# Local attention in blocks of 32 queries by 64 keys, in a six-layer transformer kernel

## The chip, the cores and the metric

The kernel runs on one core of a Trainium2 chip. The metric is the device time of one execution in microseconds (us). TensorE (PE) does the matrix products, ScalarE (ACT) activations and copies out of PSUM, VectorE (DVE) elementwise work and reductions, GpSimd (POOL) elementwise work, and the queue of SyncE (SP) issues the DMAs. PSUM has eight banks of 128 partitions by 512 fp32.

## What is computed

Eight batches of 512 tokens of 128 features pass through a full causal attention block with a layer norm, then through six layers of local attention and a gated feed-forward block, then a last layer norm. The change touches only the local attention of the six layers, 16 heads of 64 features:

```python
w = 32
bk2, bv2 = look(bk), look(bv)          # each block of 32 queries sees its own 32 keys and the 32 before
mask = (it < jb) | (it > jb + w) | (jb == -1)
sim = einsum('bhwie,bhwje->bhwij', bq, bk2) * 8.0
attn = softmax(where(mask, -max, sim), -1)
out = einsum('bhwij,bhwje->bhwie', attn, bv2)
```

A query sees itself and the 32 tokens before it, no more than 33 keys.

## The kernel before

After a first stage of about 480 us the six layers run as one software pipeline. An iteration n is one batch of one layer (48 in all); it has eight steps p = 0 to 7. A step handles a "pair": one group of four heads (a quarter of the heads) and half of the tokens (256). So there are 384 pairs. Each engine runs its own hand-written order, `cycle(n, p)`, and semaphores tie them. In step p different pairs are at different stages: the projection works on the pair of this step, the transposes of queries and keys on the pair of two steps ago (LAG_T), logits and softmax on that of four steps ago (LAG_S), transposes of the probabilities six (LAG_PT), products with the values and the output projection seven (LAG_O, LAG_Y). The feed-forward block of an older iteration (n-2) is spread over the steps: a turn at p = 2, `up` products at p = 3, 4, 6 and 7, 24 `down` products at p = 5; DVE has its layer norm at p = 0 and 1.

PE in one step, in order, with the lines of its matmuls: projection of queries and keys of the first 128 tokens (L1019 to L1021), transposes of half of the probabilities (`transpose_probs`, hp = 1, L1082), products with the values (`outputs`, L1103), logits (mask products L1118, then L1125), transposes of queries and keys (L1057), projection of the second 128 tokens (L1019 to L1021), value projection (L1031 to L1033), transposes (L1057), output projection (L1143), transposes of the other half of the probabilities (hp = 0, L1082).

Logits are made in blocks of 64 queries by 96 keys (KW = 96, so that 64 queries with their 32 older keys fit). A pair has 16 such blocks (4 heads, 4 blocks of queries). They lie in two banks as 128 partitions x 2 x 384. An fp32 matmul is recorded as two matmuls with a weight load (PEld) each, so L1125 has 32 in a step. The 64 x 64 tiles of PE that the blocks use are the four quadrants of the array. DVE takes the maxima of 128x768 (`maxima`, L1714), ACT the exponentials in eight instructions of 128x96, each with a sum (`exps`, L1441), DVE the reciprocals (L1772), POOL the products of probabilities and reciprocals (`probs`, 128x384 twice, L1564). The result PN is padded to 128 columns for each 64 queries, so two heads' blocks give one transpose of 128x128, eight in a step, in two groups of four in banks `p_ta` and `p_tb`; ACT copies each group to PT (128x512, L1402). `outputs` multiplies blocks of 64 columns of PT with values: V_odd holds the values as they were projected (128 keys), V_even a copy moved by 64 partitions by DMA (96 keys), 16 fp32 matmuls of 64 columns into one bank, `p_vo`. ACT copies that to OT (L1409).

Two loops close over a step. The logits have one pair of banks, so the masks of a pair wait until ACT has taken all eight exponentials of the pair before (`exp1`). And ACT, in its order, does: copy of probabilities (hp = 1), outputs, squares (L1417), copy of queries and keys (L1424), squares, four exponentials, copy of queries and keys, values (L1432), copy of probabilities (hp = 0), four exponentials.

Of the kernel before, what the change touches and what calls it, by code (L numbers as in the profile page):

```python
# [14 lines left out]
F32 = mybir.dt.float32  # L15
# [7 lines left out]
T = 512  # L23
# [12 lines left out]
KW = 3 * WIN  # L36
# [71 lines left out]
def first_attention(nc, dram, X, ident, banks, w, A, S, X0, kept, late):  # L108
# [3 lines left out]
    with ExitStack() as ctx:  # L112
# [56 lines left out]
        with nc.Block() as block:  # L169
# [230 lines left out]
            def _(dve):  # L400
# [18 lines left out]
                def step(b, j, odd):  # L419
# [90 lines left out]
                    if b == 7 and j == F_X + 1:  # L510
                        dve.tensor_copy(A["masks"][:, :, :], masks_f[:, :, 0:2 * KW])
                        dve.tensor_copy(A["ident_b"][:, :], ident[:, :])
# [124 lines left out]
def layer_constants(nc, ctx):  # L637
# [10 lines left out]
    sb("masks", [P, 2, 2 * KW], BF16)  # L648
# [5 lines left out]
def late_buffers(nc, ctx, A):  # L654

    both = ctx.enter_context(nc.sbuf_tensor("late", [P, 2 * NF * T + 2 * T + 6 * CQ + 16 * P + 4 * CQ + 16 * KW], F32))
# [12 lines left out]
    A["PT"] = view("layers", 16 * P, "p (s n q) -> p s n q", s=2, n=8)  # L669
    A["OT"] = view("layers", 4 * CQ, "p (s e t) -> p s e t", s=2, e=2)  # L670
# [5 lines left out]
def layer_buffers(nc, ctx, made):  # L676
# [16 lines left out]
    for n in ("V_even", "V_odd"):  # L693
        sb(n, [P, G, MT, CQ])
    sb("PN", [P, 2, 4, 2 * P])
# [41 lines left out]
def all_layers(nc, X, X0, out, ident, psum, banks, A, w, dram, S, kept, late):  # L737
# [7 lines left out]
    QK, V_even, V_odd, E, PN, negmax, esum, erec, PT, OT = (  # L745
        A[n] for n in ("QK", "V_even", "V_odd", "E", "PN", "negmax", "esum", "erec", "PT", "OT"))
# [4 lines left out]
    p_qk, p_vo, p_ta, p_tb, p_y = banks[0:2], banks[2], banks[5], banks[6], banks[7]  # L751
    p_t = (p_ta, p_tb)
    p_s = psum[:, 3:5, 0:4 * KW]
# [3 lines left out]
    end_gates, end_values, end_out = (banks[2], banks[4], banks[7]), (banks[5], banks[6], banks[0]), (banks[3], banks[1])  # L757
# [26 lines left out]
    with nc.Block() as block:  # L784

        @block.sync
        def _(sp):
            moved = {}

            def move_values(a):  # L790
# [4 lines left out]
                sp.dma_start(V_even[WIN:KW, a.g, m:m + 2, :], V_odd[0:64, a.g, m:m + 2, :]).then_inc(S[name], 16)  # L795
                later = slice(m + 1, min(m + 3, MT))
                sp.dma_start(V_even[0:WIN, a.g, later, :], V_odd[KW:P, a.g, later.start - 1:later.stop - 1, :]).then_inc(S[name], 16)
# [101 lines left out]
        def _(pe):  # L899
            def transpose_x(n):  # L900
# [3 lines left out]
                ge(pe, S["pt_out1"], done(n - 1, P_X, LAG_PT))  # L904
# [52 lines left out]
            def up(n, p, c, part, bank):  # L957
                f = n - 2
                if 0 <= f < NI:
# [3 lines left out]
                    else:  # L963
                        pe.wait_ge(S["pt_out1"], done(n, p, LAG_PT))
# [32 lines left out]
            def shifts(n):  # L997
                l = prepared(n)
                if l is not None:
                    ge(pe, S["w1"], 32 * l)  # L1000
                    ge(pe, S["pt_out1"], done(n, P_BIAS, LAG_PT))
# [34 lines left out]
            def transpose_qk(n, p, mm):  # L1036
                t = pair_at(n, p, LAG_T)
                if t:
                    f = n - 2
                    pe.wait_ge(S[f"r{mm}"], t.k + 1)  # L1040
                    ge(pe, S[f"pt_out{mm}"], done(n, p - (mm == 0), LAG_PT))
# [18 lines left out]
            def transpose_probs(n, p, hp):  # L1060
                t = pair_at(n, p, LAG_PT)
                if t:
                    f = n - 2
                    pe.wait_ge(S[f"pn{hp}"], t.k + 1)
                    pe.wait_ge(S[f"qk_out{hp}"], done(n, p - hp, LAG_T))
                    if hp == 0:
# [1014 lines left out]
```

## Time and profile before

| | |
|---|---|
| time of three runs | 3645.51 us median (3644.78 to 3646.31) |
| span of the profiled execution | 3639.9 us |
| PE, ACT, DVE, POOL busy | 3554.4, 3359.9, 3128.2, 2732.9 us |
| granted clock of PE | 9 tenths or more in all 40 slices |
| the pipeline of layers | 48 iterations of 65.6 us, eight steps each |

The page gives busy time by engine, the chain that ended last, and groups of instructions by line. The matmul records overlap each other (a matmul of 0.24 us can be followed by another 2 ns later), so a busy share of 98% says little of the rate; the chain of waits gives each group the time that it added.

### The profile page before, as it was taken

The numbers are of one execution on the slowest core, as the hardware profiler recorded it, in microseconds if no ns is written. First come the engines' busy times: TensorE is split into PE (matmuls) and PEld (weight loads), VectorE is DVE, ScalarE is ACT, GpSimd is POOL, SyncE is SP. The second block draws the span as 40 slices with busy tenths as digits, with TensorE's granted clock in tenths as the row PEclk, the third lists the DMA queues.
The fourth block names the chain that finished last, engine by engine and source line by source line (L and its number), as shares of the span: only waits on it lengthen the run. The fifth ranks groups of instructions, "written<-read, shape, count | busy, mean of one in ns | idle before, by whom it ended". The sixth has DMA issues, their size and how long they took to land.

```text
span 3639.9 us, 133048 instructions
## 1 busy us (share of the span) xinstructions
PE 3554.4 (98%) x47348; PEld 3028.6 (83%) x47348; DVE 3128.2 (86%) x7021; ACT 3359.9 (92%) x10928; POOL 2732.9 (75%) x2058
## 2 busy tenths in 40 slices
PE   8999999999999999999999999999999999999998
PEld 5666678888888888888888888888888888888887
DVE  8999988888888788887888888889888888888887
ACT  8999889999999999999999999999999999999996
POOL 0111288888888788788888888888888888888884
PEclk9999999999999999999999999999999999999999
DMA  2000011111111111111111111111111111111111
GB/s 102 7 14 10 14 38 43 35 32 34 44 43 41 28 36 36 39 46 36 33 33 40 40 45 35 33 30 43 47 35 37 30 33 45 34 35 36 42 36 39
DMA packets 165015, 132.71 MB, mean 36 GB/s; under 512 B 113933, under 2 KB 124813, under 8 KB 164109
## 3 DMA queue, kind: packets, MB, share of 16 engines
q1 hardware_dynamic: 164365, 124.19, 13.9%
q8 instruction: 390, 6.39, 0.8%
q14 instruction: 260, 2.13, 0.2%
HBM read 25.84 MB, written 4.19 MB: 8 GB/s over the span
## 4 chain that ended last, share of the span: by engine, by line
PE 75%; ACT 5%; DVE 4%; issue 3%; POOL 1%; ACTq 0%; POOLq 0%; DVEq 0%
PE bank L1103 10%; PE bank L1057 10%; PE bank L1082 8%; PE bank L1143 8%; PE bank L1125 6%; PE bank L1019 4%; PE bank L1020 4%; PE bank L1021 4%; PE bank L980 4%; PE bank L1118 3%; PE bank L953 2%; ACT late L1441 2%; PE bank L955 2%; PE bank L954 2%; PE bank L1033 2%
## 5 line engine op out<-in xcount | busy, mean ns | idle before, releaser
L1554 POOL TENSOR_TENSOR a_rn<-a_ssqc,a_minus_half 128x16 f32<-128x16 f32 x384 | 1113.2, 2899 | 490.3 <-DVE a_ssqc L1765 480.6
L1441 ACT ACTIVATE late<-bank,a_negmax 128x96 f32<-128x96 f32 x3072 | 1013.5, 363 | 11.8 <-DVE a_negmax L1714 10.7
L1577 POOL TENSOR_TENSOR a_r<-a_u,a_rn 128x512 f32<-128x512 f32 x768 | 788.3, 1046 | 0.6
L1564 POOL TENSOR_TENSOR a_PN<-late,a_erec 128x384 f32<-128x384 f32 x768 | 730.6, 971 | 9.1 <-PE bank L1082 8.2
L1441 ACT ACTIVATION_READ_ACCUMULATOR late<-bank,a_negmax 128x1 f32 x3072 | 708.7, 231 | 0.0
L1424 ACT ACTIVATE a_QK<-bank 128x512 f32<-128x512 f32 x768 | 467.8, 609 | 122.5 <-PE bank L1057 122.5
L1737 DVE TENSOR_TENSOR a_v<-bank,a_rot_s 128x512 f32<-128x512 f32 x768 | 523.1, 681 | 0.0
L1727 DVE TENSOR_TENSOR a_u<-bank,a_rot_c 128x512 f32<-128x512 f32 x768 | 521.4, 679 | 1.2 <-ACT a_sq L1417 1.1
L1417 ACT ACTIVATE a_sq<-bank 128x512 f32<-128x512 f32 x768 | 482.7, 628 | 42.2 <-PE bank L1021 12.9
L1402 ACT ACTIVATE late<-bank 128x512 f32<-128x512 f32 x758 | 479.6, 633 | 15.3 <-PE bank L1082 11.4
L1745 DVE TENSOR_TENSOR a_u<-a_u,a_v 128x1024 f32<-128x1024 f32 x384 | 489.5, 1275 | 0.7 <-issue 0.3
L1057 PE MATMUL bank<-ident,a_r 128*128 128x128 f32 x3072 | 482.4, 280 | 3.5 <-DVE a_xl L1646 2.3
L1757 DVE TENSOR_REDUCE a_ssq<-a_sq 128x16 f32<-128x1024 f32 x384 | 463.9, 1208 | 17.4 <-issue 16.7
L1082 PE MATMUL bank<-ident,a_PN 128*128 128x128 f32 x3072 | 461.2, 273 | 9.1 <-DVE X L1672 7.5
L1082 PEld LDWEIGHTS bank<-ident,a_PN 128*128 128x128 f32 x3072 | 367.2, 141 | 75.3 <-issue 30.0
L1714 DVE TENSOR_REDUCE a_negmax<-bank 128x8 f32<-128x768 f32 x384 | 365.1, 951 | 64.7 <-PE bank L1125 64.7
L1143 PE MATMUL bank<-w_out,late 128*128 128x128 f32 x3072 | 406.0, 275 | 0.0
L1103 PE MATMUL bank<-late,a_V_even 96*64 96x64 f32 x6144 | 397.6, 227 | 4.9 <-DVE late L1871 2.8
L1057 PEld LDWEIGHTS bank<-ident,a_r 128*128 128x128 f32 x3072 | 341.2, 141 | 64.8 <-issue 3.9
L1103 PE MATMUL bank<-late,a_V_odd 128*64 128x64 f32 x6144 | 379.1, 221 | 0.0
L1143 PEld LDWEIGHTS bank<-w_out,late 128*128 128x128 f32 x3072 | 373.4, 192 | 0.7 <-ACT late L1409 0.4
L1103 PEld LDWEIGHTS bank<-late,a_V_even 96*64 96x64 f32 x6144 | 310.3, 137 | 70.1 <-ACT late L1402 34.3
(191 smaller groups left out, 8129.7 us busy)
## 6 DMA issues: line engine op xcount, KB each, us to landing
a_V_even<-a_V_odd SPq DMA_DIRECT2D x384, 128.0 KB, 2.3
a_V_even<-a_V_odd SPq DMA_DIRECT2D x192, 64.0 KB, 2.2
late<-in_qkv SPq DMA_DIRECT2D x20, 384.0 KB, 3.8
a_x_sh<-X SPq DMA_DIRECT2D x48, 128.0 KB
a_V_even<-a_V_odd SPq DMA_DIRECT2D x192, 32.0 KB, 1.9
a_x_sh<-X SPq DMA_DIRECT2D x48, 127.0 KB
late<-X SPq DMA_DIRECT2D x47, 128.0 KB
late<-X SPq DMA_DIRECT2D x47, 127.0 KB
```

Source lines behind the costliest of these rows:

```text
L1057: ins = pe.transpose(p_t[mm][:, c * P:(c + 1) * P], r[:, t.par, mm * 512 + c * P:mm * 512 + (c + 1) * P], ident[:, :])
L1082: ins = pe.transpose(p_t[hp][:, i * P:(i + 1) * P], PN[:, t.par, 2 * hp + i // 2, first:first + P], ident[:, :])
L1103: ins = pe.matmul(p_vo[q, hp * CQ + i * 64:hp * CQ + (i + 1) * 64], V[:, c:c + DH], PT[keys, o.par, 4 * hp + i, side:side + 64], start=Tru ...
L1143: ins = pe.matmul(p_y[:, i * P:(i + 1) * P], OT[:, y.par, hp, mm * P:(mm + 1) * P], w.out[:, 2 * y.g + hp, :], start=(y.pos + hp == 0 and ...
L1417: act.activation(sq[:, mm * 512:(mm + 1) * 512], p_qk[mm][:, :], ACT.Square).then_inc(S[f"sq{mm}"], 1)
L1441: ins = act.activation(E[:, s.par, k, :], scores[:, i % 2, col:col + KW], ACT.Exp, bias=negmax[:, s.par, k:k + 1], accum_out=esum[:, s.par ...
L1554: pool.tensor_tensor(rn[:, a.par, :], ssqc[:, a.par, :], minus_half[:, :], ALU.pow).then_inc(S["rn"], 1)
L1564: pool.tensor_tensor(PN[:, s.par, 2 * hp:2 * hp + 2, :].rearrange("p i (b k) -> p i b k", b=2)[:, :, :, 0:KW], spread(E[:, s.par, half, :] ...
L1577: pool.tensor_tensor(heads(r[:, a.par, half]), heads(u[:, a.par, half]), rn[:, a.par, mm * 2 * HG:(mm + 1) * 2 * HG].unsqueeze(2).to_broad ...
L1727: dve.tensor_tensor(view(u[:, a.par, mm * 512:(mm + 1) * 512]), view(p_qk[mm][:, :]), tab, ALU.mult).then_inc(S["u_rot"], 1)
L1737: dve.tensor_tensor(halves(v[:, mm * 512:(mm + 1) * 512]), halves(p_qk[mm][:, :])[:, :, :, ::-1, :], tab, ALU.mult).then_inc(S[f"v_rot{mm} ...
L1745: dve.tensor_tensor(u[:, a.par, :], u[:, a.par, :], v[:, :], ALU.add).then_inc(S["u"], 1)
```

## The change

KW becomes 64: logits are blocks of 32 queries by 64 keys, 32 blocks in a pair, each in a tile of 64 rows by 32 columns of the array. They take 128 partitions x 2 x 256 of PSUM, even heads in one bank and odd heads in the other. Masks are eight bf16 products of 32 rows by 256 columns. Maxima, exponentials and probabilities get two thirds of the elements, with the same number of instructions. PN is [128, 4, 128] without padding: each 128x128 block, four in a step, is transposed once, into `p_ta` alone; one copy by ACT gives PT. `outputs` has 32 fp32 matmuls of 64 keys by 64 features by 32 queries, in the four quadrants of the array; the results of keys in the lower 64 partitions go to `p_vo`, the others to `p_tb`, and ACT copies both banks in one instruction. `p_vo` and `p_ta` exchange banks. The values lie in V_nat (as projected) and V_sh (moved down by 32 partitions by DMA): the first of two DMAs for a pair moves 96 partitions instead of 64.

```diff
-KW = 3 * WIN
+KW = 2 * WIN
...
-                sp.dma_start(V_even[WIN:KW, a.g, m:m + 2, :], V_odd[0:64, a.g, m:m + 2, :]).then_inc(S[name], 16)
+                sp.dma_start(V_sh[WIN:P, a.g, m:m + 2, :], V_nat[0:P - WIN, a.g, m:m + 2, :]).then_inc(S[name], 16)
...
+            def prob_transposes(t):
+                for k in range(4):
+                    ins = pe.transpose(p_ta[:, k * P:(k + 1) * P], PN[:, t.par, k, :], ident[:, :])
+                ins.then_inc(S["pt"], 1)
...
+                    pe.wait_ge(S["qk_out1"], keys_out)
                     ge(pe, S["o_out"], o.k)
...
                     for hp in range(2):
-                        for i in range(4):
-                            keys = slice(0, P if i % 2 else KW)
-                            V = (V_odd if i % 2 else V_even)[keys, o.g, 2 * o.half + i // 2, :]
-                            for e in range(2):
-                                q, c, side = slice(64 * e, 64 * e + 64), hp * P + 64 * e, 64 * ((e + i) % 2)
-                                ins = pe.matmul(p_vo[q, hp * CQ + i * 64:hp * CQ + (i + 1) * 64], V[:, c:c + DH],
-                                                PT[keys, o.par, 4 * hp + i, side:side + 64], start=True, stop=True)
+                        for c in range(4):
+                            m, own = divmod(c, 2)
+                            V, col = V_nat if own else V_sh, hp * P + c * WIN
+                            for half in range(2):
+                                keys = slice(KW * half, KW * half + KW)
+                                for e in range(2):
+                                    q, v = slice(64 * e, 64 * e + 64), hp * P + 64 * e
+                                    ins = pe.matmul(p_o[half][q, col:col + WIN], V[keys, o.g, 2 * o.half + m, v:v + DH],
+                                                    PT[keys, o.par, 2 * e + hp, c * WIN:(c + 1) * WIN], start=True, stop=True,
+                                                    skip_group_check=True)
...
+                    for c in range(4):
+                        for e in range(2):
+                            rows = slice(WIN * c, WIN * c + WIN)
+                            pe.matmul(scores[rows, e, :], ident_b[sides[e], 64 * e:64 * e + WIN],
+                                      masks[sides[e], int(s.half > 0 or c > 0), :], start=True, stop=True, skip_group_check=True)
                     for hp in range(2):
...
+                        for half in range(2):
+                            col = (2 * hp + half) * KW
+                            for c in range(4):
+                                first = (2 * s.half + c // 2) * P + half * KW + c % 2 * WIN
+                                for e in range(2):
+                                    ins = pe.matmul(scores[WIN * c:WIN * c + WIN, e, col:col + KW],
+                                                    QK[sides[e], s.gpar, hp, WIN + first:WIN + first + WIN],
+                                                    QK[sides[e], s.gpar, 2 + hp, first:first + KW], start=False, stop=True,
+                                                    skip_group_check=True)
...
                 project(n, p, 0)
-                transpose_probs(n, p, 1)
-                outputs(pair_at(n, p, LAG_O), n * NP + p)
+                if p == P_GELU + 1:
+                    ge(pe, S["f_out"], n - 2)
+                outputs(pair_at(n, p, LAG_O), n * NP + p, done(n, p - 1, LAG_T))
...
                 transpose_qk(n, p, 1)
+                transpose_probs(n, p)
                 output_projection(pair_at(n, p, LAG_Y))
-                transpose_probs(n, p, 0)
...
-                probs(t, 1)
+                squares(n, p, 0)
                 outputs(o)
-                squares(n, p, 0)
...
-                probs(t, 0)
+                probs(t)
```

Where PE waited for `pt_out1` before writing `p_tb` (transposes of keys, `up`, x), it now waits for `o_out`. The last steps, written out one by one in `end()`, follow the same rules.

## Rows read from the trace of the kernel before

**Rows 1.** The page: span, busy time, and the granted clock in 40 slices.

```profile
span 3639.9 us, 133048 instructions
PE 3554.4 (98%) x47348; PEld 3028.6 (83%) x47348; DVE 3128.2 (86%) x7021; ACT 3359.9 (92%) x10928; POOL 2732.9 (75%) x2058
...
PEclk9999999999999999999999999999999999999999
```

**Rows 2.** The page: the chain that ended last, share by engine.

```profile
PE 75%; ACT 5%; DVE 4%; issue 3%; POOL 1%; ACTq 0%; POOLq 0%; DVEq 0%
```

**Rows 3.** The chain of waits over one step (start, time added, what), step p = 0.

```profile
2069.33 0.44 PE bank L1082 x4
2069.76 1.08 PE bank L1103 x32
2070.85 0.29 PE bank L1118 x8
2071.14 0.66 PE bank L1125 x32
```

**Rows 4.** Timeline of PE (start, us, what): step p = 0 and the next masks.

```profile
2068.38 0.48 PE L1019 MATMUL bank<-a_wh,a_xh 128*128 128x512 f32 x1
...
2069.69 0.34 PE L1103 MATMUL bank<-late,a_V_even 96*64 96x64 f32 x4
...
2070.78 0.36 PE L1118 MATMUL bank<-a_masks,a_ident_b 64*64 64x192 bf16 x8
...
2071.73 0.66 PE L1057 MATMUL bank<-ident,a_r 128*128 128x128 f32 x4
...
2075.31 0.48 PE L1019 MATMUL bank<-a_wh,a_xh 128*128 128x512 f32 x1
...
2076.62 0.34 PE L1103 MATMUL bank<-late,a_V_even 96*64 96x64 f32 x4
...
2077.81 0.36 PE L1118 MATMUL bank<-a_masks,a_ident_b 64*64 64x192 bf16 x8
```

**Rows 5.** Windows of 5 ns on L1125's matmuls: stretch, length, busy, running (x).

```profile
2004.94:2004.95 0.01, 0.01 (x4) 1.00 0.23 51
2004.96:2004.96 0.01, 0.01 (x8) 1.00 0.00 0
2005.02:2005.03 0.01, 0.01 (x8) 1.00 0.23 51
2005.04:2005.05 0.01, 0.01 (x12) 1.00 0.23 51
```

**Rows 6.** Timeline of PE: matmuls of one column, then the projection.

```profile
507.51 1.25 PE L1006 MATMUL bank<-w_cols,w_w 128*128 128x1 f32 x12
508.62 0.48 PE L1019 MATMUL bank<-a_wh,a_xh 128*128 128x512 f32 x1
```

**Rows 7.** Timeline of ACT over the same step as rows 4.

```profile
2072.42 0.60 ACT L1424 ACTIVATE a_QK<-bank 128x512 f32<-128x512 f32 x1 [0.41 <-PE bank L1057]
2073.12 0.60 ACT L1417 ACTIVATE a_sq<-bank 128x512 f32<-128x512 f32 x1
2073.61 0.33 ACT L1441 ACTIVATE late<-bank,a_negmax 128x96 f32<-128x96 f32 x1
...
2074.87 0.62 ACT L1424 ACTIVATE a_QK<-bank 128x512 f32<-128x512 f32 x1
...
2076.30 0.39 ACT L1441 ACTIVATE late<-bank,a_negmax 128x96 f32<-128x96 f32 x1
```

**Rows 8.** Busy time by engine: steps p = 7, 0, 1, then p = 5, 6.

```profile
2060.40:2082.50 22.10, 22.07 (x334) 19.76 (x333) 21.84 (x44) 20.50 (x74) 18.95 (x15) 1.00 0.19 46
2041.30:2060.40 19.10, 18.66 (x250) 16.37 (x248) 12.54 (x20) 17.86 (x52) 13.85 (x10) 1.00 0.12 28
```

**Rows 9.** Groups by line from 600 to 3500 us: busy, mean ns, idle before.

```profile
L1714 DVE TENSOR_REDUCE a_negmax<-bank 128x8 f32<-128x768 f32 x353 | 335.7, 951 | 58.1 <-PE bank L1125 58.1
L1757 DVE TENSOR_REDUCE a_ssq<-a_sq 128x16 f32<-128x1024 f32 x353 | 426.5, 1208 | 16.8 <-issue 16.1
```

More of the change, by code:

```diff
@@ L647, in layer_constants @@
         sb(n, [P, MT, 2, DH])
-    sb("masks", [P, 2, 2 * KW], BF16)
+    sb("masks", [P, 2, 4 * KW], BF16)
     sb("ident_b", [P, P], BF16)
@@ L692, in layer_buffers @@
     sb("QK", [P, 2, 4, XC])
-    for n in ("V_even", "V_odd"):
+    for n in ("V_sh", "V_nat"):
         sb(n, [P, G, MT, CQ])
-    sb("PN", [P, 2, 4, 2 * P])
+    sb("PN", [P, 2, 4, P])
     for n in ("negmax", "esum", "erec"):
@@ L903, in transpose_x @@
                 ge(pe, S["h"], NF * (n - 3) + 1)
-                ge(pe, S["pt_out1"], done(n - 1, P_X, LAG_PT))
+                ge(pe, S["o_out"], done(n - 1, P_X, LAG_O))
                 for i in range(MT):
@@ L963, in up @@
                     else:
-                        pe.wait_ge(S["pt_out1"], done(n, p, LAG_PT))
+                        pe.wait_ge(S["o_out"], done(n, p, LAG_O))
                     if part == 0:
@@ L1000, in shifts @@
                     ge(pe, S["w1"], 32 * l)
-                    ge(pe, S["pt_out1"], done(n, P_BIAS, LAG_PT))
+                    ge(pe, S["o_out"], done(n, P_BIAS, LAG_O))
                     pe.wait_ge(S["xl"], n + 1)
@@ L1040, in transpose_qk @@
                     pe.wait_ge(S[f"r{mm}"], t.k + 1)
-                    ge(pe, S[f"pt_out{mm}"], done(n, p - (mm == 0), LAG_PT))
+                    if mm == 0:
+                        ge(pe, S["pt_out"], done(n, p - 1, LAG_PT))
+                    else:
+                        ge(pe, S["o_out"], done(n, p, LAG_O))
                     if n == 0:
@@ L1286, in end_outputs @@
             def end_outputs(j):
-                outputs(end_pair(j), NI * NP)
+                outputs(end_pair(j), NI * NP, NI * NP + min(0, j + 5))
             def end_projection(j):
@@ L1329, in end @@
                 end_up(0, 1)
+                end_probs(-1)
                 end_projection(-2)
-                end_probs(-1, 0)
                 end_up(1, 1)
@@ L1984, in _ @@
             end()
-LAYER_SEMS = ("xt xh xl x_loaded f_loaded qk_out0 qk_out1 pt0 pt1 pt_out0 pt_out1 v_out o_out o y pn0 pn1 exp0 exp1 logits r0 r1 "
+LAYER_SEMS = ("xt xh xl x_loaded f_loaded qk_out0 qk_out1 pt pt_out v_out o_out o y pn0 pn1 exp0 exp1 logits r0 r1 "
               "qkt0 qkt1 sq0 sq1 qk v max red u u_rot rec0 rec1 rn v_rot0 v_rot1 summed x_out weights w_hi w_lo raw0 raw1 scales "
```

171 lines of the change are left out of this document (64 added, 107 removed).

## The prediction

> **What bounds the kernel now.** I read the page first, then the chain of waits, then one step on each engine. The page [rows 1] shows PE busy 98% of the span at an undiminished clock and ACT at 92%: two engines without reserve. The chain [rows 2] is PE for 75%. But matmul records overlap, so the price of a PE group has to come from the time that it adds to the chain [rows 3]: transposes of probabilities 0.44 us for each group of four (two groups a step), products with the values 1.08, masks and logits 0.29 + 0.66. Together 2.91 us of a plain step (p = 0) of 6.93 us, which is the distance of the two first L1019 [rows 4].
>
> A second bound lies close behind. From one pair's masks to the next are 7.03 us [rows 4], and this can be walked through ACT [rows 4, 7]: masks to transposes of keys 0.95 (2070.78 to 2071.73), to their copy on ACT 0.69, to the squares 0.70 (they wait for the projection), to the first exponential 0.49, four exponentials 1.26, copies of keys, values and probabilities 1.43, and from the second four to the next masks 1.51. The sum is 7.03: the masks wait for `exp1` and nothing else is slack. The masks start 1.19 us after the first product with the values at p = 1 (2076.62 to 2077.81) and 1.09 at p = 0 [rows 4]: only the former waits 0.1 us for the exponentials. The other steps repeat one of these, p = 2 to 4 the former and p = 5 to 7 the latter, so I count four turns as bound by the loop and four by PE.
>
> A third is DVE. Over steps p = 7, 0 and 1, where it also has the norm's statistics and the last residual sums, it is busy 21.84 of 22.10 us; over p = 5 and 6 only 12.54 of 19.10 [rows 8].
>
> **The change, part by part, per step.**
>
> Transposes of probabilities. One group of four of two goes: 0.44 us of PE [rows 3]. The tile change before the outputs is still there, it only follows the projection. The group that stays is moved ahead of the output projection, which costs nothing by itself; what queues behind it (projection, in step 5 the `down` products) needs it done either way. One ACT copy of 128x512 goes too; it stood between `exp1` and the squares, where ACT then waits 0.41 us for keys anyway [rows 7], so I cost it at nothing. If that wait closed, it would be worth up to 0.48.
>
> Logits. The 32 recorded matmuls of 96 columns become 64 of 64 columns. The price depends on how many the array runs at once. Windows of 5 ns [rows 5] show the matmuls start in groups of four: 4 records are open at 2004.94 and 8 some 0.01 us later, still 8 at 2005.02 and 12 at 2005.04. So four start within about 0.01 us and then none until the next four; 8 such rounds are the 0.66 of [rows 3], 0.082 us each, with one matmul in each quadrant. Four starts close together after a pause mean that the array, not the issue of instructions, sets the pace. 0.082 us for 96 columns; by proportion 0.055 for 64. With tiles of 64 rows by 32 columns there is room for eight at once, and the written order takes all eight tiles in turn: 64 / 8 = 8 rounds of 0.056 = 0.45, a saving of 0.21. If only four run at once it is 16 rounds, 0.90, a loss of 0.24. No row shows eight tiles. I take eight, because the rounds of [rows 5] are already full, one matmul in every tile that exists there, and keep both ends.
>
> Masks. Eight matmuls of 192 columns take two rounds (0.19 us between the L1118 and L1125 starts, about 0.11 and 0.08). Eight of 256 columns in eight tiles take one, about 0.13: 0.05 saved; two rounds of four would take 0.24: 0.05 lost.
>
> Products with the values. 32 recorded matmuls of 64 columns become 64 of 32 columns, two tiles at once become four. Each still loads 64 columns of weights, and a load has its price where matmuls have one column [rows 6]: 12 of them, eight with 128 and four with 85 columns of weights (the chunks of 341), take 1.11 us, 0.81 ns a column, so 64 columns 0.052 and about 0.058 with what is between two. Now 16 rounds of 0.058 make 0.93 of the 1.08; afterwards 64 / 4 = 16 rounds, bound by the load instead of the matmul, 0.93 again: no change. That loads of four tiles overlap follows from [rows 5]: 4 x 0.052 would not fit in 0.082. The upper end is a round of 0.082, the slowest that four tiles show: 16 x 0.024 = 0.38 more. Below zero it can't go far, as the loads bound it.
>
> PE in sum: -0.44 - 0.21 - 0.05 = -0.70, with ends -0.80 (a cheaper tile change) and +0.23.
>
> A rule of the Trainium skill speaks against this. The page "TensorEngine Tiling (Array Packing)", section "Instruction Overhead", says that each matmul carries about 60 cycles, that one of a single column takes as long as one of 60, and that a tiling factor shouldn't be taken from a dimension that is small already. An estimate from that page's figure is 64 x 25 ns = 1.6 us for the outputs and as much for the logits, against 0.93 and 0.66 now. The rows show four matmuls starting within about 10 ns; that speaks for a pace set by tile, not by instruction.
>
> Softmax. ACT: an instruction with 96 columns takes 0.33 and one with 512 takes 0.60 [rows 7], 0.65 ns a column; 32 columns fewer are 0.021, eight times 0.17 us, all in the loop. DVE: maxima cost 1208 ns for 1024 columns and 951 for 768 [rows 9], 1.0 ns a column, so 256 fewer give 0.26. POOL has a third less in its two products; it is busy 18.95 of 22.10 [rows 8] and not the end of any walk above, so nothing is counted.
>
> Added waits. The outputs now fill `p_tb` as well, so the transposes of keys (second half), `up` at p = 3, 4, 6 and x at p = 7 wait for ACT's copy of the outputs. ACT makes it second after `exp1`, about 0.15 + 2 x 0.48 = 1.1 us later; PE needs masks, logits and key transposes, 0.69 + 0.41 = 1.1, before the earliest of them (p = 3 and 7). Cost nothing to 0.1 in two steps of eight; I take nothing. Outputs wait also for `qk_out1` of the step before, done four exponentials earlier. The DMA of values moves 96 partitions for 64, and has seven steps.
>
> **The sum.** The loop gets shorter by 0.26 (masks and logits) + 0.17 (exponentials) = 0.43, to 6.60 us; PE alone would need 6.23. So of the 0.70 a turn that the loop bounds gives only 0.43. By stretches (7, 0, 1 and 5, 6 as in [rows 8]): p = 5 and 6, PE bound, 2 x 0.70 = 1.40. p = 2 to 4: two turns by the loop and one by PE, 0.43 + 0.43 + 0.70 = 1.56. p = 7, 0, 1: PE and loop would give 0.6 + 0.43 + 0.43 = 1.46, but DVE has 0.26 idle and saves 3 x 0.26: 1.04; I take 1.1. In sum 4.06 us of the 65.6 of an iteration, x 48 = 195 us. Against the profiled span: 3640 - 195 = 3445. The median of the runs lies 5.6 us above the span, and that stays: 3450 us.
>
> **Rivals.**
> 1. Eight tiles don't run at once, or the issue holds a round of eight to twice its length. Then logits and masks cost 0.29 more a step: PE -0.44 + 0.29 = -0.15, loop +0.29 - 0.17 = +0.12. Four turns of each: -0.1 us an iteration, 5 us in all: 3640, with 3620 to 3660 around it. For it: no row shows more than four tiles.
> 2. The forecast's mechanism with dearer products with the values (rounds of 0.082): +0.38 on PE. The loop's turns hide it (6.23 + 0.38 = 6.61), the four PE turns don't: 4.06 - 4 x 0.38 = 2.5 us, 3640 - 120 + 6 = 3526.
> 3. The other side: matmuls have a pace of their own. They never come closer than 82 / 4 = 20.6 ns on average in [rows 5]. If that is a floor of decoding or fetching (each has a weight load beside it), the outputs cost 64 x 20.6 = 1.32 (+0.39) and the logits 1.32 (+0.66), the transposes still give 0.44: +0.61 a step, PE bound throughout, 8 x 0.61 x 48 = 234 us: 3880. It decides from 16 ns a matmul upward: 128 x 16.3 ns is the 0.93 + 0.66 + 0.44 + 0.05 that is to be had. Against it: the groups of four in [rows 5]. This is also the direction of the page's rule.
> 4. DVE doesn't bind and the loop is all: 4.42 us, 3434; PE's full 0.70 in every step would be 3377.
>
> **Chances.** Forecast with its own spread 0.56, rival 2 (and mild forms, with rounds of 0.06 to 0.08) 0.12, rival 1 0.14, rival 3 0.14, others 0.04. The forecast's own range is 3395 to 3490. The range that holds 8 in 10 must take in rivals 2 and 1, so 3390 to 3650. A measurement of this kernel tells some 0.2% (7 us) from no change: faster 0.73, within 0.10 (most of rival 1), slower 0.17.
>
> **What would show it.** In the changed kernel's chain, logits at 0.45 us (right), 0.90 (rival 1) or 1.3 (rival 3), outputs near 1.08 for 64 records or 1.5; one group of transposes of 0.44. In narrow windows on the logits eight should start together. Plain steps should be about 6.6 us from masks to masks, with PE idle some 0.3 us ahead of them on ACT's exponentials. DVE should stay near 98% over p = 7, 0, 1. If PE had no such idle time and steps were 6.2, the loop was read wrongly.

## The result, and the profile after

The changed kernel takes 3823.65 us (median of four runs, 3821.83 to 3827.0), beside 3645.15 of the kernel before (four runs, 3641.79 to 3646.31): a ratio of 1.0492, 95% interval 1.0479 to 1.0505. It is 179 us slower, where 195 us less had been forecast, and it lies outside the range of 3390 to 3650. The profiled execution took 3827.0, its span 3825.2.

The page of the changed kernel: span and busy times (these answer to [rows 1]), the queue that brings instructions, and the chain by engine (this answers to [rows 2]).

```profile
span 3825.2 us, 178160 instructions
PE 3474.8 (91%) x70388; PEld 2895.0 (76%) x70388; DVE 3009.8 (79%) x7016; ACT 3101.7 (81%) x10549; POOL 2561.0 (67%) x2057
...
q8 instruction: 569, 9.32, 1.0%
...
PE 51%; issue 13%; ACT 12%; DVE 10%; POOL 2%; ACTq 0%; DVEq 0%; POOLq 0%
```

The same queue on the page of the kernel before (packets, MB, share):

```profile
q8 instruction: 390, 6.39, 0.8%
```

No engine is as busy as it was (ACT fell most, from 92% to 81%), and yet the span grew. The chain says where to look: PE fell from 75% to 51%, and "issue", time in which the engine waited for nothing that the profile shows, rose from 3% to 13%. The second thing to see is the queue of instructions: 569 fetches where there were 390.

The waits of PE from 600 to 3500 us say which lines (waiting line, releaser: us in total, times, longest). First the changed kernel, then the one before.

```profile
PE bank L1129 <- issue: 131.8, 102, 2.5
PE bank L1083 <- DVE late L1651: 32.6, 84, 0.5
PE bank L1061 <- issue: 21.4, 14, 2.2
PE bank L1083 <- ACT late L1369: 18.0, 42, 0.4
PE bank L1106 <- ACT late L1398: 17.9, 113, 0.2
PE bank L1083 <- DVE a_f_xl L1640: 13.6, 35, 0.8
```

```profile
PE bank L953 <- DVE late L1664: 10.3, 44, 0.3
PE bank L1082 <- DVE X L1672: 7.3, 44, 0.2
PE bank L953 <- ACT late L1373: 7.3, 44, 0.2
```

Two new things stand there. Inside the logits (L1129), and sometimes at the transposes of keys behind them (L1061), PE stands still for up to 2.5 us with nothing to wait for. And the transposes of probabilities (L1083) now wait for the feed-forward part (L1651 products, L1369 gate, L1640 low half of x), which they did not do in the old place.

The timeline of PE in the changed kernel (start, us, what): an undisturbed logits stretch, which answers to [rows 4], and the next one, which is disturbed.

```profile
2060.06 0.30 PE L1121 MATMUL bank<-a_masks,a_ident_b 64*32 64x256 bf16 x8
2060.18 0.84 PE L1129 MATMUL bank<-a_QK 64*32 64x64 f32 x64
2060.95 0.66 PE L1061 MATMUL bank<-ident,a_r 128*128 128x128 f32 x4
...
2067.71 0.30 PE L1121 MATMUL bank<-a_masks,a_ident_b 64*32 64x256 bf16 x8
2067.83 0.40 PE L1129 MATMUL bank<-a_QK 64*32 64x64 f32 x25
2070.06 0.88 PE L1129 MATMUL bank<-a_QK 64*32 64x64 f32 x39 [1.83 <-issue]
2070.86 1.11 PE L1061 MATMUL bank<-ident,a_r 128*128 128x128 f32 x4
...
2075.73 0.60 PE L1061 MATMUL bank<-ident,a_r 128*128 128x128 f32 x4
2076.75 0.63 PE L1083 MATMUL bank<-ident,a_PN 128*128 128x128 f32 x4 [0.43 <-ACT late L1369]
```

The masks take 0.12 us and the logits 0.77, up to the next group. In the second stretch 25 of the 64 matmuls run, then nothing for 1.83 us, then the other 39. In the last two lines the transposes of probabilities come 1.02 us after those of keys instead of 0.44.

Windows of the changed kernel over the disturbed stretch (stretch, length, busy time and count of PE, PEld, DVE, ACT, POOL, then the granted clock, DMA share, GB/s):

```profile
2064.00:2067.90 3.90, 3.70 (x103) 3.11 (x109) 2.71 (x7) 3.90 (x20) 3.22 (x3) 1.00 0.18 49
2067.90:2070.00 2.10, 0.33 (x33) 0.16 (x17) 1.10 (x1) 0.73 (x2) 2.10 (x3) 1.00 0.09 25
2070.00:2072.00 2.00, 1.94 (x44) 1.77 (x45) 1.03 (x2) 0.00 (x0) 2.00 (x3) 0.53 0.03 8
2072.00:2076.00 4.00, 3.85 (x18) 2.96 (x18) 2.88 (x6) 3.03 (x12) 0.08 (x2) 0.81 0.00 0
```

After PE has stood still the granted clock is 0.53 of full, that is the lower level of 1.2 GHz for nearly the whole window, and only comes back within the window behind it (0.81). The four transposes at 2070.86 last 1.11 us instead of 0.66. In the whole trace there are 36 stretches at the lower level, 146 us together; before the change there was one of 4 us. 32 of the 36 follow a standstill of over 0.6 us before another step has passed.

**Where PE stands still.** I numbered all of PE's records in the trace in order of time, weight loads and matmuls each for one: 145,694, which is 569 x 256 but for 30; in the kernel before 99,814, or 390 x 256 but for 26. So one fetch of queue q8 (9.32 MB / 569 = 16 KB) brings 256 instructions. Between 600 and 3500 us PE stood still 100 times for over 0.6 us without a releaser, and all 100 fall at the same remainder of 256: at the border of two such blocks. A gap is from here on the time from the last record of a block to the first of the next, if it is over 0.2 us. The changed kernel has 182 gaps, 229 us together; before there are 13, together 3 us.

The starts of the q8 packets tell more, read over the 509 borders behind 676 us. Call lead the time from the start of a block's fetch until PE reaches the block. No block was used sooner than 2.15 us after that start. Of the 140 borders with a lead under 2.2 us 138 have a gap, of the 369 with more 31. At the 123 gaps of over 0.6 us the time from the landing of the packet to the block's first use is 1.39 us (median; 1.23 to 1.52 for eight of ten), the packet itself takes 0.92 to 1.65 (eight of ten again), and the gap is what the lead lacks to their sum.

The fetch starts some 156 records ahead of the border (median), which is little where these are short. In the kernel before no lead of 339 is under 2.2, and nine of ten are over 5.6 us. One step now has outputs, masks and logits in a row: 64 + 8 + 64 matmuls with as many loads, 272 instructions in 1.96 us. Before it was 144 in 2.04 (2069.69 to 2071.73, [rows 4]).

**Times by step.** From one first projection to the next (L1020, before L1019), medians over the iterations of the steady part, p = 0 to 7: 6.43, 7.16, 8.06, 7.33, 9.15, 9.28, 9.13, 8.17 us, in sum 64.7; before 6.93, 7.03, 7.74, 7.74, 8.80, 9.88, 9.16, 8.06, in sum 65.3. By the mean, which takes in the standstills, 69.6 against 65.6. The mean's difference times 48 iterations is 191 us, as much as the whole result (the spans differ by 185). So there are two questions: why the median steps gain 0.6 us an iteration and not 4.1, and why the mean now lies 4.9 us above the median, 4.6 more than before.

### The profile page after: what moved, and what is told of

The parts are those of the page before. It is cut to its first block, busy times and chain, and to the rows that moved or that the text cites. A ratio compares the mean times of both kernels' runs of the same rounds, so it can differ in the third digit from the quotient of the medians.

```text
span 3825.2 us, 178160 instructions
## 1 busy us (share of the span) xinstructions
PE 3474.8 (91%) x70388; PEld 2895.0 (76%) x70388; DVE 3009.8 (79%) x7016; ACT 3101.7 (81%) x10549; POOL 2561.0 (67%) x2057
## 3 DMA queue, kind: packets, MB, share of 16 engines
q8 instruction: 569, 9.32, 1.0%
## 4 chain that ended last, share of the span: by engine, by line
PE 51%; issue 13%; ACT 12%; DVE 10%; POOL 2%; ACTq 0%; DVEq 0%; POOLq 0%
PE bank L1106 7%; PE bank L1129 7%; PE bank L1061 7%; ACT late L1436 6%; PE bank L1147 5%; PE bank L1083 3%; DVE a_ssq L1744 3%; PE bank L981 3%; PE bank L1020 3%; PE bank L1022 3%; PE bank L1021 3%; DVE late L1651 2%; PE bank L1121 2%; ACT a_V_nat L1427 2%; ACT late L1398 2%
## 5 line engine op out<-in xcount | busy, mean ns | idle before, releaser
L1436 ACT ACTIVATE late<-bank,a_negmax 128x64 f32<-128x64 f32 x3072 | 931.4, 336 | 9.4 <-DVE a_negmax L1701 8.9
L1554 POOL TENSOR_TENSOR a_PN<-late,a_erec 128x256 f32<-128x256 f32 x768 | 561.9, 749 | 16.2 <-DVE a_erec L1759 7.6
L1061 PE MATMUL bank<-ident,a_r 128*128 128x128 f32 x3072 | 497.5, 285 | 32.0 <-issue 24.0
L1744 DVE TENSOR_REDUCE a_ssq<-a_sq 128x16 f32<-128x1024 f32 x384 | 465.9, 1213 | 75.1 <-issue 67.8
L1129 PE MATMUL bank<-a_QK 64*32 64x64 f32 x24576 | 354.5, 223 | 153.1 <-issue 152.9
L1732 DVE TENSOR_TENSOR a_u<-a_u,a_v 128x1024 f32<-128x1024 f32 x384 | 471.0, 1227 | 0.7 <-issue 0.3
L1106 PEld LDWEIGHTS bank<-late,a_V_sh 64*64 64x64 f32 x12288 | 325.8, 134 | 181.0 <-ACT late L1398 100.2
L1129 PEld LDWEIGHTS bank<-a_QK 64*32 64x32 f32 x24576 | 306.6, 106 | 166.6 <-issue 166.0
L1701 DVE TENSOR_REDUCE a_negmax<-bank 128x8 f32<-128x512 f32 x384 | 264.4, 688 | 210.6 <-PE bank L1129 209.0
L1061 PEld LDWEIGHTS bank<-ident,a_r 128*128 128x128 f32 x3072 | 352.2, 144 | 90.8 <-issue 42.3
L1106 PE MATMUL bank<-late,a_V_sh 64*64 64x32 f32 x12288 | 391.4, 222 | 29.6 <-ACT late L1398 23.3
L1106 PE MATMUL bank<-late,a_V_nat 64*64 64x32 f32 x12288 | 383.6, 219 | 0.0
L1020 PE MATMUL bank<-a_wh,a_xh 128*128 128x512 f32 x768 | 370.9, 483 | 5.6 <-DVE a_v L1724 4.7
```

Of the source, the lines that this page charges most:

```text
L1020: pe.matmul(p_qk[mm][:, :], xh[:, x, m], wh[:, a.g, 0:2 * CQ], start=True, stop=False)
L1061: ins = pe.transpose(p_t[mm][:, c * P:(c + 1) * P], r[:, t.par, mm * 512 + c * P:mm * 512 + (c + 1) * P], ident[:, :])
L1106: ins = pe.matmul(p_o[half][q, col:col + WIN], V[keys, o.g, 2 * o.half + m, v:v + DH], PT[keys, o.par, 2 * e + hp, c * WIN:(c + 1) * WIN], ...
L1129: ins = pe.matmul(scores[WIN * c:WIN * c + WIN, e, col:col + KW], QK[sides[e], s.gpar, hp, WIN + first:WIN + first + WIN], QK[sides[e], s. ...
L1436: ins = act.activation(E[:, s.par, k, :], scores[:, hp, col:col + KW], ACT.Exp, bias=negmax[:, s.par, k:k + 1], accum_out=esum[:, s.par, k ...
L1554: pool.tensor_tensor(PN[:, s.par, 2 * hp:2 * hp + 2, :].rearrange("p i (b k) -> p (i b) k", b=2), E[:, s.par, half, :], erec[:, s.par, hal ...
```

## The experiments

Theories: **M**, the moved transposes cost waits. **I**, the logits are bound by the issue of instructions and no longer by the array. **F**, the fetch of instruction blocks can't follow a dense stretch, and PE stands still at block borders. Rival to F: the standstills come from something else at that place (the array, a wait that the profile doesn't show).

**One: the changed kernel with the output projection back ahead of the transposes.**

```diff
                 transpose_qk(n, p, 1)
-                transpose_probs(n, p)
                 output_projection(pair_at(n, p, LAG_Y))
+                transpose_probs(n, p)
```

> The changed kernel with one move undone: output projection ahead of the transposes of probabilities, as before. In the changed kernel PE waits 0.53, 0.59, 0.66 and 0.44 us at p = 2, 4, 6 and 7 between its last key transposes and the transposes of probabilities (0.96, 1.03, 1.10, 0.88 from start to start, against 0.44 elsewhere), for copies and sums by ACT and DVE that the projection (0.81 us) used to cover. Theory M (this move costs its waits): 2.2 us an iteration, 106 us in all, 3718 us. Rival (the waits come back at another place, or the time is lost in PE's instruction supply only): 3790 us or more.

Measured: 3798.51 us beside 3645.12, ratio 1.0416 (1.0399 to 1.0433): 25 us better than the change, far less than M's 2.2 us an iteration (106 us), and within what had been set for the rival (3790 or more). The waits of PE in this kernel:

```profile
PE bank L1129 <- issue: 146.6, 101, 2.9
PE bank L1106 <- ACT late L1398: 22.7, 137, 0.3
PE bank L1061 <- issue: 19.0, 12, 2.1
```

All waits of L1083 are gone, as M says. But the sum of the medians fell by only 1.1 us an iteration, to 63.6: the transposes are later, so ACT's copy of them (L1398) is later and the outputs (L1106) wait for it more often. And the gaps rose from 229 to 248 us, the lower clock from 146 to 191. The change has too many other losses to weigh this one in it, so I made the same move in the kernel before.

**Two: the kernel before, with the second group's transposes ahead of the output projection.** The move that I had costed at nothing, alone.

```diff
                 transpose_qk(n, p, 1)
-                output_projection(pair_at(n, p, LAG_Y))
                 transpose_probs(n, p, 0)
+                output_projection(pair_at(n, p, LAG_Y))
```

> The kernel before with nothing changed but the second group of transposes of probabilities ahead of the output projection, as the changed kernel has it. Theory M: the projection no longer covers what those transposes wait for (the turned input at p = 2, gates at p = 4, products at p = 6 and 7); PE gets the waits that the changed kernel shows, up to 2.2 us an iteration, of which some is regained where PE waited later anyway: 60 to 106 us more, 3705 to 3750. Rival (PE loses nothing by itself, as the prediction had it): within 20 us of 3645.

Measured: 3743.16 us beside 3644.09, ratio 1.0270 (1.0253 to 1.0287): 99 us for one swapped line. Its page and PE's waits:

```profile
span 3741.7 us, 133048 instructions
PE 3585.0 (96%) x47348; PEld 3029.5 (81%) x47348; DVE 3118.6 (83%) x7021; ACT 3383.5 (90%) x10928; POOL 2737.9 (73%) x2058
...
PE bank L1082 <- DVE late L1664: 33.2, 86, 0.5
PE bank L1082 <- ACT late L1373: 21.7, 42, 0.5
PE bank L1082 <- DVE a_f_xl L1653: 15.5, 43, 0.4
```

The same three waits as in the changed kernel, with nearly the same totals, in a kernel with no more instructions than before: 14 gaps, 4 us. At p = 2, 4, 6 and 7 the transposes come 0.88 to 1.12 us after those of keys, elsewhere 0.44. Median and mean of an iteration agree (67.7 and 67.8). The time lies in the expected 3705 to 3750: M is shown, with its price.

**Three: half as many key columns.** The changed kernel; each logits matmul takes 32 of its 64 columns (the other half of the scores is left out), and the count of instructions stays.

```diff
-                                    ins = pe.matmul(scores[WIN * c:WIN * c + WIN, e, col:col + KW],
+                                    ins = pe.matmul(scores[WIN * c:WIN * c + WIN, e, col:col + WIN],
                                                     QK[sides[e], s.gpar, hp, WIN + first:WIN + first + WIN],
-                                                    QK[sides[e], s.gpar, 2 + hp, first:first + KW], start=False, stop=True,
+                                                    QK[sides[e], s.gpar, 2 + hp, first:first + WIN], start=False, stop=True,
```

> The changed kernel with 32 instead of 64 columns in each logits matmul (the second half of the keys is left out of the scores), same number of instructions. Theory I (a matmul and its weight load need 16.7 ns of issue, and logits are bound by that once the queue ahead is used up): from the first logits matmul to the next transposes stays 0.775 us, the time within 15 us of 3824. Rival (array bound): that stretch falls by 0.2 us, the time by up to 80 us.

Measured: 3815.16 us (one run). In the timeline of this kernel, an undisturbed stretch and a disturbed one:

```profile
2051.33 0.75 PE L1129 MATMUL bank<-a_QK 64*32 64x32 f32 x64
2052.01 0.66 PE L1061 MATMUL bank<-ident,a_r 128*128 128x128 f32 x4
...
2059.03 0.37 PE L1129 MATMUL bank<-a_QK 64*32 64x32 f32 x25
2061.25 0.68 PE L1129 MATMUL bank<-a_QK 64*32 64x32 f32 x39 [1.85 <-issue]
```

Half the columns shortened the stretch from 0.775 to 0.677 us: neither not at all, as I says, nor by the 0.2 us of the rival. The standstill has the same place, after 25 matmuls, and the same length. The starts say more. With 64 columns (the changed kernel) every fourth matmul starts at 0, 13, 56, 69, 112, 168, 188, 243, 308, 341, 391, 424, 458, 491, 533, 569 ns (medians): first eight for each 56 ns, and from about the 32nd on four for each 33 to 42 ns. With 32 columns the first sixteen start 3.5 ns apart, and then it is four for each 33.3 ns again. So the second half of the stretch has a pace that does not depend on the columns: 8.35 ns for a matmul with its load. I holds there, with half the price that I had expected of an instruction pair, and not in the first half. That the first half runs from what had been queued up while the outputs were slower is my reading; no run varied it. The loads were the same in both kernels, 32 columns, so this run alone can't tell a pace of issue from one of loading; experiments five and six can. The time fell by only 8.5 us, with the lower clock at 233 us for 146; what that took of it I can't say.

**Four: half as many logits.** The changed kernel, `for hp in range(1)` in place of `range(2)`: the scores of two of four heads are left out, and 32 matmuls with their loads a step.

> The changed kernel without the logits of half of the heads (32 matmuls and 32 weight loads fewer in a step; those heads get masks only). Theories I and F: 32 x 16.7 ns = 0.4 to 0.53 us less a step in the steps that PE bounds, and gaps at block borders fall from 229 to under 110 us with the clock above 0.99: about 3600 us. Rival to F: the gaps stay near 229 us and the time falls by no more than 100 us.

Measured: 3551.05 us (one run), 273 us less than the change. On its page:

```profile
span 3549.3 us, 153584 instructions
...
q8 instruction: 473, 7.75, 0.9%
```

96 fetches fewer, and 96 x 256 = 24,576 is just the count of records left out, 64 x 384. Gaps: 74, 82 us in sum instead of 229; lower clock 72 us instead of 146. From the first logits to the transposes of keys it is 0.461 us for 0.775, which is 121 us over 384 steps, and the gaps give 147: together 268 of the 273. The gaps stay under F's 110 us, the 0.31 us a step is less than I's 0.4 to 0.53, and the time is 50 us under the 3600 that I expected. The standstills shrank with the number of instructions, which speaks for F, but this run takes array work away as well.

**Five and six: instructions without work in the kernel before.** 32 (then 64) matmuls of one bf16 column with their loads behind the logits of each step, in a part of two banks that nothing reads: dense instructions, in a kernel that had none of the gaps and in which all else is as before.

```diff
+                    for k in range(pad):
+                        e, i = k % 2, k // 2 % 2
+                        q = sides[e]
+                        ins = pe.matmul(psum[sides[(e + i) % 2], 3 + i, 500:501], ident_b[q, q], masks[q, 1, 0:1], start=True,
+                                        stop=True, skip_group_check=True)
                     ins.then_inc(S["logits"], 1)
```

> The kernel before, with 32 added bf16 matmuls of one column behind the logits of each step (64 instructions more in a step, results in unused columns of PSUM). Theories I and F: the pads add 32 x 16.7 ns = 0.53 us a step of issue, 205 us, and the dense stretch of 208 instructions makes gaps at block borders appear, 20 to 120 us (3 us in the kernel before): 3870 to 3970 us. Rival to F (gaps belong to the 32-column tiles or the new waits): no gap above 0.6 us, 3850 us or less. Rival to I (matmuls of different tiles are issued 2 to 4 ns apart): pads add under 0.2 us a step, 3720 us or less.

> As e5_before_with_pads with 64 instead of 32 one-column matmuls, so 128 instructions more in a step, as many as the change adds. e5 had gaps at block borders of 51 us, and its pads took 8 ns each. Theory F: the dense stretch now has 272 instructions like the changed kernel's, gaps of 150 to 280 us, with the clock below 0.99; and 64 x 8 ns = 0.51 us a step of issue, 0.26 more than in e5, 100 us: 3960 to 4100 us. Rival (gaps grow only in proportion to the instructions): about 100 us of gaps, 3920 us or less.

Measured with 32: 3783.23 us (one run), 138 more than before, below the expected 3870, as the pads cost half of what I had put. Gaps: 80, together 51 us (20 to 120 expected), 41 of them over 0.6 us, where the rival to F had none. The pads themselves take 254 ns in a step, 8 ns each, and lengthen the median of an iteration by 2.0 us. Measured with 64: 3980.67 us (one run), 337 more, inside the expected band; gaps: 163, together 133 us, which is under the 150 that F should have made, and the mean clock of 0.994 isn't under 0.99. Of 135 borders with a lead under 2.2 us 133 have a gap. The timeline of PE in the kernel with 64, a disturbed step, and its waits:

```profile
2009.43 0.83 PE L1126 MATMUL bank<-a_QK 64*64 64x96 f32 x32
2010.09 0.57 PE L1133 MATMUL bank<-a_masks,a_ident_b 64*64 64x1 bf16 x50
2011.61 0.29 PE L1133 MATMUL bank<-a_masks,a_ident_b 64*64 64x1 bf16 x14 [0.95 <-issue]
...
PE bank L1133 <- issue: 75.4, 95, 1.7
PE bank L1058 <- issue: 8.8, 10, 1.6
```

The standstill is there, in the kernel before, at the border of a block, and where it comes (after 50 pads) there is nothing to wait for. From none to 32 to 64 pads the gaps go 3, 51, 133 us: F is shown apart from the change's tiles, data and DMAs, with less gap time than I had expected. The mean is above the median by 1.1 us an iteration with 32 pads and by 2.6 with 64, which times 48 is 52 and 123 us, close to the gaps. The lower clock took 19 and 48 us there. What it costs by itself I can't say: no run had the one without the other.

The pads' starts also settle I. With 64 of them the first 26 come in rounds of four, a round every 31.6 ns, and from the 31st on one comes every 8.3 ns, evenly, to the last (medians). It is the pace of the logits' second half, where the loads were 32 fp32 columns and the tiles 64 x 32; here they are 64 bf16 columns and the tiles 64 x 64, with a single column to multiply. A pace that stays while load, tile and columns change fits the issue of instructions and not the array.

**Seven to nine: thinning the dense stretch in the changed kernel.** If F holds, the same instructions with slower work in between should stall less. Seven puts the second projection between outputs and logits:

```diff
                 outputs(pair_at(n, p, LAG_O), n * NP + p, done(n, p - 1, LAG_T))
+                project(n, p, 1)
                 if s:
                     ge(pe, S["exp1"], s.k)
...
                     transpose_x(n + 1)
-                project(n, p, 1)
```

with ACT's second squares ahead of its copy of keys, and DVE's first cosines ahead of the maxima, to fit. Eight is seven with the swap of experiment one. Nine is experiment one with the logits and the wait for `exp1` moved behind the second projection:

```diff
-                if s:
-                    ge(pe, S["exp1"], s.k)
-                logits(s, p_s)
                 transpose_qk(n, p, 0)
...
                 project(n, p, 1)
+                if s:
+                    ge(pe, S["exp1"], s.k)
+                logits(s, p_s)
```

with DVE's maxima behind its first cosines and sines.

> The changed kernel with the second projection of queries and keys (three matmuls, 0.78 us, six instructions) moved between outputs and logits, and the first key transposes behind the logits (ACT's squares and DVE's first rotation follow). Same instructions, same work. Theory F: gaps at block borders fall from 229 us to 90 to 150, because the last 150 instructions before a border then rarely pass in under 2.2 us; the loop through ACT stays 6.5 us, so nothing new waits; 3700 to 3760 us. Rival (the gaps belong to tiles or waits): gaps stay above 200 us and the time above 3790.

> Both e7_second_projection_between and the output projection ahead of the transposes of probabilities. In e1 the latter took PE's waits of 2.2 us an iteration away and gave half of them back as waits of the outputs for ACT's copy of the probabilities (0.2 to 0.3 us a step). Theory: 30 us less than e7, 3670 to 3730. Rival (the outputs' wait for the copy grows as the exponentials come later): not faster than e7.

> As e1_projection_first, and the logits are moved behind the second projection of queries and keys (DVE's maxima behind the first two rotations), so that the two dense stretches of short matmuls, outputs and logits, have 1.2 us with few instructions between them. Number of instructions and their work are the same. Theory F (PE's instructions are fetched in blocks of 256, a block can be used 2.2 us after its fetch starts, and the dense stretch of 272 instructions uses the old block up before): the gaps at block borders, 229 us of the changed kernel, fall below 60, the clock returns to 0.995 or more, and the time is 3450 to 3560 us. Rival (the gaps are waits for other engines, or come from small tiles themselves): gaps stay above 150 us and the time within 60 us of e1_projection_first.

Measured:

| kernel | us | ratio (95%) | gaps: us | lower clock: us | iteration: median, mean |
|---|---|---|---|---|---|
| the change | 3823.65 | 1.0492 (1.0479 to 1.0505) | 229 | 146 | 64.7, 69.6 |
| one | 3798.51 | 1.0416 (1.0399 to 1.0433) | 248 | 191 | 63.6, 69.2 |
| seven | 3790.70 | 1.0401 (1.0386 to 1.0417) | 124 | 31 | 67.1, 68.7 |
| eight | 3767.40 | 1.0328 (1.0311 to 1.0345) | 146 | 54 | 65.9, 68.2 |
| nine | 3754.34 | 1.0301 (1.0286 to 1.0317) | 78 | 65 | 66.2, 67.8 |

The gaps fall as the stretch is thinned, by up to two thirds, and that part of F holds once more: 124 us in seven, where 90 to 150 was expected, but 78 in nine, where I had put under 60. The times all came out above what I expected, 3700 to 3760 for seven, 3670 to 3730 for eight and 3450 to 3560 for nine: each order pays elsewhere, and none comes near 3645. Eight is 23 us better than seven, as forecast (30). In nine only one of the 16 stretches at the lower clock follows a gap of over 0.6 us. PE's waits in nine:

```profile
PE bank L1106 <- ACT late L1398: 69.6, 198, 2.4
PE bank L1129 <- issue: 46.4, 64, 2.1
PE bank L907 <- ACT late L1404: 26.4, 43, 1.3
PE bank L954 <- ACT late L1404: 22.4, 43, 1.2
```

With logits later, maxima and exponentials are later, and with them ACT's copies of the probabilities (L1398) and outputs (L1404). The last two are the added waits for `o_out` (x at p = 7 and `up` at p = 3) that the prediction had costed: here they are 49 us together, in the change's own order they don't appear. In seven a new wait of 32.7 us for the copy of keys stands before L949 (the turn of p = 2).

## Why the prediction was wrong

Its steps in turn.

- **Transposes, -0.44 us a step: right.** One group of four is left, and its median is 0.44. At p = 0, which neither waits nor is loop-bound, the step went from 6.93 to 6.43. The parts add up: -0.44 (transposes), -0.07 (masks), -0.02 (outputs), +0.01 (logits) give -0.52 against -0.50 measured.
- **"Moved ahead of the output projection, which costs nothing by itself": wrong, about 2.1 us an iteration.** I had looked at what queues behind the group on PE and not at what it waits for, for each value of p. The group writes the bank `p_ta`, which the feed-forward part has used just before: the turned x at p = 2 (L1640 reads it), `up` at p = 4 (ACT's gate, L1369) and at 6 and 7 (DVE's products, L1651). The output projection, 0.89 us from its start to that of the transposes behind it, was the cover, and the prediction named no work that would hide the waits once it was gone. Before: L1082 waited 7.3 us over 2900; after: L1083 64 us (32.6 + 18.0 + 13.6). Experiment two prices it at 99 us, half of the whole forecast gain.
- **Masks, one round of 0.13: right** (0.12).
- **Logits, 8 rounds of 0.056 = 0.45: wrong in size, 1.7 us an iteration.** From the first logits to the transposes of keys it is 0.775; before it was 0.76 ([rows 4]: 0.95 from the masks on, less the 0.19 of the masks), and with the forecast saving of 0.21 it would have been 0.55. The mechanism was half right: eight tiles do run at once. Windows of 5 ns on L1129 in the changed kernel (stretch, length, busy, running, clock, DMA share, GB/s), which answer to [rows 5]:

```profile
2060.20:2060.20 0.01, 0.01 (x8) 1.00 0.19 43
...
2060.23:2060.24 0.01, 0.01 (x8) 1.00 0.00 0
...
2060.26:2060.26 0.01, 0.01 (x16) 1.00 0.23 51
...
2060.28:2060.29 0.01, 0.01 (x16) 1.00 0.19 43
```

  Eight open, a pause, eight more after 0.056: the round is as I had sized it. But it is kept up only over the first 20 or so matmuls. From about the 32nd on matmuls with their loads come at 8.35 ns a pair, 0.067 us for eight. [rows 5] could not show this, as four pairs in each 0.082 us stay far from that pace. Four starts close together show that the issue is fast enough for four; they say nothing on eight for every 0.056 us.
- **Outputs, no change: right.** 64 matmuls start over 916 ns, where 32 took 932, in rounds of 58.3 ns for four, which is the 0.058 that [rows 6] gave for the load of the weights. Rival 2 falls.
- **The ACT copy that goes, at nothing: right as far as it goes, but its other half isn't free.** All probabilities are now transposed in one group, and the outputs follow the projection at once. They wait for the one copy (L1398) at p = 1, 2, 4 and 6, 0.16 to 0.23 us each by the medians.
- **Softmax: DVE right, ACT a bit high.** Maxima 688 ns for 951 [rows 9]: 0.26. The exponentials' mean went from 363 to 336 ns, 0.027 each, 0.21 us a step for 0.17.

```profile
L1436 ACT ACTIVATE late<-bank,a_negmax 128x64 f32<-128x64 f32 x3072 | 931.4, 336 | 9.4 <-DVE a_negmax L1701 8.9
...
L1701 DVE TENSOR_REDUCE a_negmax<-bank 128x8 f32<-128x512 f32 x384 | 264.4, 688 | 210.6 <-PE bank L1129 209.0
```

  DVE's maxima now idle 209 us for the logits, 65 before: with those waits DVE is busy about 91% over p = 7, 0 and 1 (ten iterations, standstills included), and that part of the sum (near 98%) did not come about.
- **The loop through ACT: read rightly, worth less.** At p = 1, 2 and 4 the masks still come 0.05 us after the last exponential, as before, and then 0.12 us later behind the outputs than in the other steps; forecast was some 0.3. From masks to masks p = 0 and 1 take 6.77 and 6.81 us, 7.03 before, 6.60 by the forecast: the dearer logits lie in the loop too.
- **Added waits for `o_out`, nothing: right in this order,** and wrong as soon as the logits are later (nine).
- **What the prediction didn't have at all: the supply of instructions.** PE's records go from 99,814 to 145,694, and nothing in it asks what more instructions in the same time would do beyond their issue. 229 us of gaps and the lower clock behind them are the largest term. The page of the kernel before had a row for it, the 390 fetches of q8, and its trace had 13 small gaps with 3 us; I had read neither.

The terms, over the whole run: forecast -195; logits +81 (0.21 x 8 x 48); moved transposes +99; standstills and what follows them 4.6 x 48 = +220. The sum is +205, measured by the spans +185. The 20 us too many may be overlap (a standstill also hides a wait that would have come) and the better exponentials; no run separates them.

The rivals: one's first form (eight tiles don't run at once) fell with the windows above; its second, that issue holds a round back, is of the right kind, but 0.067 us for eight is far from twice 0.056. Counted from logits to transposes its 0.90 stands for 1.00 and my 0.45 for 0.55, and the measured 0.775 lies halfway. Three (a pace of their own, 3880) came nearest to the time, for another reason: the pace is 8.35 ns and not 20.6, below the 16 from which it should have decided, and the rest is supply and order. The page "TensorEngine Tiling (Array Packing)" of the Trainium skill, section "Instruction Overhead", says of small dimensions not to tile them, with 60 cycles for each matmul. Its advice agrees with the result; its price doesn't: an estimate from its figure, 64 x 25 ns, would be 1.6 us, and the rows have 0.77.

## What to carry to other kernels

Count instructions as well as columns. Where a change doubles the matmuls of a stretch, compare the time in which PE goes through some 150 records there with the 2.2 to 2.5 us that a new block of 256 needed here, and look in the trace of before for PE's gaps that have no releaser. And an edit that moves an instruction ahead of another "at no cost" is to be checked for what the moved one waits for, in every variant of the step, with the work that it leaves behind taken as its cover; here one line was worth 99 us.

## What was not expected of the hardware

- PE's instructions arrive in blocks of 256 (16 KB), and in the changed kernel no block was used sooner than 2.15 us after its fetch began. At gaps of over 0.6 us it was 2.5 us (median): the packet and 1.39 us more. The constant is the same in the kernel before with pads (1.39 at 107 gaps with 64 of them, 1.39 at 40 with 32). The packet isn't constant, and where it is late the block is as much late (correlation 0.93 over the 123 gaps). In the disturbed stretch shown above it took 1.44 us, beside data that filled the DMA engines. Against the 0.92 of the fastest tenth the packets took 0.29 us more in the mean; x 123 that makes 36 us, my estimate of what other DMA traffic, the values' among it, has to do with the 229. No run varied that.
- Matmuls of small tiles with their loads came every 8.3 ns where a dense stretch had run on for some 30 of them, with 64, 32 or one column alike. The first sixteen of a stretch came 3.5 ns apart (32 columns, experiment three). The page "TensorE: Matmul & The Clock Gate" of the Trainium skill, in the section "Wait — 56ns, not 53.3ns?", says that starts never come closer than about 25 ns; the trace doesn't agree where successive matmuls go to different tiles. Its section "Measured speedup vs the span model", with about 4 ns of issue for each tile, does agree with the first sixteen.
- Whether the lower clock level follows a standstill of PE goes with its length. In the changed kernel it followed within a step at 26 of the 38 gaps of over 2.0 us, at 5 of the 38 between 1.5 and 2.0, and at 3 of the 106 shorter ones. With 32 pads only one of 80 gaps was over 1.5 us, and one stretch followed a gap of over 0.6. Length isn't all: in experiment one it was 23 of the 59 gaps between 1.5 and 2.0 us. What else decides the runs don't show.
